# Two fused attentions: steps grouped in blocks of two, and the maxima's matmuls spread over seven places of a block

## What is computed

```python
# A: 8 heads, latent of 32, per head 128 + 32 dimensions
c_q = h @ W_DQ + b_DQ ; c_kv = h @ W_DKV + b_DKV
scores = einsum('bhsd,bhtd->bhst', q, k) * scale ; o = softmax(scores) @ v_c
A = o.reshape(b, s, 1024) @ W_O + b_O
# B: 16 heads of 16 dimensions, keys masked by a similarity to a global token
pos = sim > 0.9
x_pos = masked_attn(pos) ; x_neg = masked_attn(~pos)       # masked softmax
B = where(pos, x_pos, x_neg) @ W_proj + b_proj             # the first 5 tokens: their mean
```

## Time and profile before

| | us |
|---|---|
| median of 3 runs | 3412.9 (3410.66 to 3431.38) |
| span of the profiled execution | 3409.3 |
| PE busy | 3051.9 (90%) |
| DVE busy | 2265.2 (66%) |
| ACT busy | 1709.1 (50%) |
| POOL busy | 1060.2 (31%) |
| PE waiting for DVE's maxima, at the maxima of B (L1008) | 75.9 in matmuls, 309.2 in weight loads |

### The profile page before, as it was taken

One profiled execution on the slowest core, in us unless ns is written; L12 is line 12 of the kernel. 1 busy time (PEld: TensorE's weight loads), 2 busy tenths in 40 slices (PEclk: granted clock), 3 DMA queues, 4 the chain that ended last, 5 costly groups with the idle time before them and its releaser, 6 DMA issues.

```text
span 3409.3 us, 47004 instructions
## 1 busy us (share of the span) xinstructions
PE 3051.9 (90%) x17538; PEld 1327.5 (39%) x17538; DVE 2265.2 (66%) x4088; ACT 1709.1 (50%) x1948; POOL 1060.2 (31%) x552
## 2 busy tenths in 40 slices
PE   5538898999989998999989998999989999899997
PEld 4423433344333433344333433344333433344333
DVE  4435466776767667776767667776767667676782
ACT  1211354654555454654555454654555455654565
POOL 1021451235222451235222451235222451235201
PEclk8765999999999999999999999999989999999998
DMA  3212421450034201450034301450034201550001
GB/s 116 89 49 69 95 52 41 106 107 17 28 83 99 60 22 47 106 104 18 28 83 97 62 19 50 105 105 18 28 83 96 64 18 37 117 107 15 19 15 33
DMA packets 130051, 213.54 MB, mean 63 GB/s; under 512 B 48376, under 2 KB 76952, under 8 KB 129688
## 3 DMA queue, kind: packets, MB, share of 16 engines
q1 hardware_dynamic: 125480, 202.24, 24.9%
q10 hardware_dynamic: 4352, 8.39, 0.7%
HBM read 137.28 MB, written 73.02 MB: 62 GB/s over the span
## 4 chain that ended last, share of the span: by engine, by line
PE 75%; DVE 16%; issue 3%; DMA 3%; POOL 2%; ACT 1%; SPq 0%; DVEq 0%; POOLq 0%; ACTq 0%
PE O L1104 22%; PE M L1008 14%; DVE mx L1310 13%; PE M L1002 8%; PE S L1092 7%; PE S L1089 4%; PE M L1028 3%; PE M L1118 3%; PE M L1069 2%; PE M L974 2%; PE M L1037 2%; PE M L1071 2%; PE M L1024 1%; DMA kt_d<-stg 1%; PE M L1033 1%
## 5 line engine op out<-in xcount | busy, mean ns | idle before, releaser
L1310 DVE TENSOR_REDUCE mx<-M 128x1 f32<-128x512 f32 x3072 | 1975.6, 683 | 742.0 <-PE M L1008 443.8
L862 ACT ACTIVATE PT<-S 128x1024 f32<-128x1024 f32 x1280 | 1269.1, 1023 | 881.7 <-PE S L1092 572.9
L1008 PE MATMUL M<-KB,QB 50*128 50x512 f32 x2048 | 684.2, 488 | 129.4 <-DVE mx L1310 75.9
L1008 PEld LDWEIGHTS M<-KB,QB 50*128 50x128 f32 x2048 | 281.2, 189 | 796.2 <-issue 395.6
L1104 PE MATMUL O<-PT,VB 128*32 128x512 f32 x4096 | 562.9, 622 | 0.7 <-ACT PT L862 0.7
L1092 PE MATMUL S<-QB,KB 52*128 52x512 f32 x2048 | 527.1, 448 | 2.4 <-ACT PT L862 2.1
L1002 PE MATMUL M<-KA,QA 98*128 98x512 f32 x1024 | 449.8, 479 | 38.8 <-DVE mx L1310 15.5
L746 POOL TENSOR_TENSOR PT<-PT 128x2048 f32<-128x2048 f32 x64 | 292.2, 4566 | 381.9 <-PE O L1104 364.7
L862 ACT ACTIVATE PTx<-S 128x1024 f32<-128x1024 f32 x256 | 248.5, 1022 | 249.0 <-PE S L1089 248.9
L746 POOL TENSOR_TENSOR PTx<-PTx 128x2048 f32<-128x2048 f32 x64 | 292.2, 4566 | 228.8 <-PE O L1104 228.8
L1002 PEld LDWEIGHTS M<-KA,QA 98*128 98x128 f32 x1024 | 182.8, 195 | 352.6 <-issue 193.4
(11 more groups left out here) (146 smaller groups left out, 1940.0 us busy)
## 6 DMA issues: line engine op xcount, KB each, us to landing
qk_d<-stg SPq DMA_DIRECT2D x32, 1024.0 KB
KA<-kt_d SPq DMA_DIRECT2D x48, 512.0 KB, 7.3
QB<-qk_d SPq DMA_DIRECT2D x192, 128.0 KB
KB<-qk_d SPq DMA_DIRECT2D x192, 128.0 KB
kt_d<-stg SPq DMA_DIRECT2D x16, 1024.0 KB
RB<-recb_d SPq DMA_DIRECT2D x64, 256.0 KB
PT<-in_x SPq DMA_DIRECT2D x16, 512.0 KB, 3.8
xn_d<-xnT ACTq DMA_DIRECT2D x16, 512.0 KB, 2.8
```

The costliest lines, as they stand in the source:

```text
L862: nc.scalar.activation(probs(kind, of_a)[:, 2 * pair:2 * pair + 2, :], Sg[pair][:, :].rearrange("p (j s) -> p j s", j=2), ACT.Exp, scale=S ...
L1008: done = mm(m[:, :], QB[rows, 2 * q + a, at:at + P], KB[rows, 2 * q + a, keys], start=True, stop=True)
L1310: v.tensor_reduce(mx[:, g % 2, unit, kh:kh + 1], m[:, :], AX.X, ALU.max).then_inc(free, 1)
```

## The change

The loops run over blocks of two steps (RUN = 2). A block's part list has seven places; its eight maxima are spread over them by SPREAD, for all four stages alike: u0 and u1 ahead of the first scores, u2, u3, u4 each ahead of one further pair of scores, u5 ahead of the first values, u6 and u7 between the two values, none at the end. PE's order in a block is

```diff
+RUN = 2
+SPREAD = ((0, 2), (2, 3), (3, 4), (4, 5), (5, 6), (6, 8))
+MID = 2
 def place(s, at, kind, nxt):
     units = max_units(kind, nxt)
-    for i in range(NC):
-        step, (u0, u1, u2, u3) = s[at + i], units[4 * i:4 * i + 4]
-        ...
+    for i in range(NC // RUN):
+        u = units[4 * RUN * i:4 * RUN * (i + 1)]
+        for part, (lo, hi) in enumerate(SPREAD):
+            s[at + i][part] = u[lo:hi] + s[at + i][part]
...
-THREE = 3
+THREE = 2 // RUN
...
-    def probs(kind, k):
-        if kind == "a":
-            return (PT if k % 4 < 2 else PTx)[:, k % 2]
-        return PT[:, k % 2]
+    def probs(k):
+        return (PT if k % 4 < 2 else PTx)[:, k % 2]
...
         def add_pair(n, i):
             k = 2 * i + 1
-            wait_apart(pool, pv_done, n * STEPS + k)
+            if n or i:
+                wait_apart(pool, dn_done, n * PAIRS + i)
             wait_apart(pool, e_done, n * (2 * STEPS) + (2 * k + 2))
-            to = probs("a", k - 1)
-            nc.gpsimd.tensor_tensor(to, to, probs("a", k), ALU.add).then_inc(summed, 1)
+            nc.gpsimd.tensor_tensor(SUM[:, :, :], probs(k - 1), probs(k), ALU.add).then_inc(summed, 1)
...
         def b_steps(b, last):        # ACT
-            for k in range(STEPS_B):
-                exps(b, STEPS_A + k, "b")
-                if k == 0:
-                    take_out(b, "a", GA - 1)
-                ...
-                fills(sum(slots[k], []), lambda j: b_spot(b, last, j), b + 1)
+            for d in range(BLOCKS_B):
+                fills(slots[d][0], lambda j: b_spot(b, last, j), b + 1)
+                for i in range(2 * RUN):
+                    exps(b, STEPS_A + RUN * d + i // 2, "b", i % 2)
+                    fills(slots[d][i + 1], lambda j: b_spot(b, last, j), b + 1)
+                ...
+                if d == 0:
+                    take_out(b, "a", GA - 1)
...
-            for e in range(2):
+            for e in ((0, 1), (1, 0))[pair]:
...
         def b_steps(b, last):        # PE
-            for k in range(STEPS_B):
-                scores(b, k, "b", 0)
-                some(k, 0)
-                scores(b, k, "b", 1)
-                some(k, 1)
-                if k:
-                    values(b, k - 1, "b")
-                ...
-                some(k, 2)
+            for d in range(BLOCKS_B):
+                for i in range(2 * RUN):
+                    some(d, i)
+                    scores(b, RUN * d + i // 2, "b", i % 2)
+                for i in range(RUN):
+                    some(d, 2 * RUN + i)
+                    if d:
+                        values(b, RUN * (d - 1) + i, "b")
+                    ...
+                if RUN * (d + 1) == 2:
+                    denominators(b, b, PAIRS - 1)
+                some(d, PARTS - 1)
```

More of the change, by code:

```diff
@@ L97, in jobs_b @@
-    if more:
[L98 to L102, removed]
+            s[(g * NC + 1) // RUN][MID].append(("fa", "a", 0))
+    s[6 // RUN][MID] += [("rs", 0), ("rs", 1)]
+    s[10 // RUN][MID] += [("rt", 0), ("rt", 1)]
+    s[12 // RUN][MID] += [("rv", 0)]
+    for c, at in enumerate((44, 46, 52, 54)):
+        s[at // RUN][MID].append(("po", c))
@@ L103, in jobs_b @@
+    if more:
+        s[14 // RUN][MID] += [("lat", 0), ("lat", 1)]
+        s[18 // RUN][MID] += [("va", 0)]
+        for at, name in ((20, "kt0"), (24, "kb"), (28, "kt1"), (34, "qk0"), (40, "qk1"), (48, "qk2"), (58, "qk3")):
+            s[at // RUN][MID].append((name, 0))
+            s[(at + 2) // RUN][MID].append((name, 1))
     for g in range(GB):
         if g + 2 < GB:
-            place(s, g * NC, "b", g + 2)
+            place(s, g * GROUP, "b", g + 2)
         elif more:
-            place(s, g * NC, "a", g + 2 - GB)
+            place(s, g * GROUP, "a", g + 2 - GB)
@@ L583, in load_z @@
                 wait_apart(sp, ld_b[q], b * LD_B + LD_B)
-            wait_apart(sp, z_clear, b + 1)
+            if b:
+                wait_apart(sp, sr_ready, b)
             for e in range(2):
@@ L642, in b_steps @@
             for g in range(GB):
+                if g + 1 < GB:
+                    shift(b, "b", g + 1, b_spot(b, last, ("fa", "b", g + 1)))
+                elif not last:
+                    shift(n, "a", 0, b_spot(b, last, ("fa", "a", 0)))
                 if g:
@@ L646, in b_steps @@
                     dens(b, "a", GA - 1)
-                if g + 1 < GB:
-                    shift(b, "b", g + 1, b_spot(b, last, ("fa", "b", g + 1)))
-                elif not last:
-                    shift(n, "a", 0, b_spot(b, last, ("fa", "a", 0)))
                 if g == 0:
@@ L1135, in some @@
                     job(j, a_spot(n, b, j), b if j[0] == "po" else n, b)
-            for k in range(STEPS_A):
-                scores(n, k, "a", 0)
-                some(k, 0)
-                scores(n, k, "a", 1)
-                some(k, 1)
-                if k:
-                    values(n, k - 1, "a")
-                elif before:
-                    values(b, STEPS_B - 1, "b")
-                if k >= 3 and k % 2 == 1:
-                    denominators(n, b, (k - 3) // 2)
-                some(k, 2)
+            for d in range(BLOCKS_A):
+                for i in range(2 * RUN):
+                    some(d, i)
+                    scores(n, RUN * d + i // 2, "a", i % 2)
+                for i in range(RUN):
+                    some(d, 2 * RUN + i)
+                    if d:
+                        values(n, RUN * (d - 1) + i, "a")
+                    elif before:
+                        values(b, STEPS_B - RUN + i, "b")
+                if RUN * d >= 2 and RUN * (d + 1) % 2 == 0:
+                    denominators(n, b, RUN * (d + 1) // 2 - 2)
+                some(d, PARTS - 1)
         def b_steps(b, last):
@@ L1175, in _ @@
         b_steps(B - 1, True)
-        values(B - 1, STEPS_B - 1, "b")
+        for i in range(RUN):
+            values(B - 1, STEPS_B - RUN + i, "b")
         for j in TAIL:
```

161 lines of the change are left out of this document (70 added, 91 removed).

## The result

| | before | after |
|---|---|---|
| median of four runs each, us | 3414.2 (3410.66 to 3431.38) | 3495.3 (3486.36 to 3498.34) |
| ratio, 95% interval | | 1.0226 (1.0197 to 1.0254) |
| span of the profiled execution, us | 3409.3 | 3495.5 |
| TensorE's granted clock, mean over the span (the view of cores) | 0.945 | 0.929 |

The changed kernel is slower by 2.3%. The time lies inside the forecast range, and slower had the largest chance, but the forecast was 3444: of the 82 us above the 3412.9 that it started from, 31 were forecast.

What follows compares the result with a forecast made beforehand. PE held 75% of the chain; in B/b a PE-DVE loop was the bound. Full batch -10.3 + 7.0 + 6.0 + 0.6 = +3.3, seven times +23, last +10.6: +34 on 3412.9 is 3446, taken as 3444; range 3350 to 3510.

Steps and rivals of the forecast that it cites:

- The plain B/b block: B/b blocks without a job: two exponentials in a row set 5.92 us, for 5.86 before, +0.06 a block.
- the plain block of B/a: B/a: added changes of tile shape take two steps from 5.98 to 6.86 us, +0.88 a block, +7.0 a batch.
- The rival of cheap changes: B/a and A/b: a lone matmul costs 0.23, not 0.44, so both stages stay even; 3347 us, chance 0.1.
- that of DVE as the bound: B/b: exponentials overlap better, a block falls to DVE's 4.96 and a little, 5.3; 3330 us, chance 0.1.
- the sum of B/b: B/b in a full batch: plain blocks, job places, fa, start of B and kb stall together -10.3 us.
- -0.43 a job place: B/b: PE's idle time hides part of each job, saving 0.43 us at 15 places, 6.5 a batch.
- -0.35 an fa: B/b: each of six transposes fa vanishes in the wait, saving about 0.35 us, 2.0 a batch.
- -1.2 at B's start: Start of B: maxima further apart, so the missing bank no longer costs; some -1.2 us a batch.
- -2.0 at kb: B/b: kb's eviction waits for kt0's store; DVE reaches the reciprocal about 1.4 us earlier, taken as -2.0.
- J + 5.11: B/b: V1 to V1 of a block with a job of length J, so J - 0.81 over a plain 5.92.
- the jobs are not covered: B/b: a projection's eviction on ACT delays the block's later exponentials, losing the 6.5 and 2.0; 3508 us, chance 0.2.
- The last batch: Final batch: B/b -4, A +6.6, tail of 8 blocks without maxima +8 (4.9 us a block), together +10.6 us.

Runs made afterwards that it cites:

- half exponentials: Changed kernel with B's exponentials over half of the columns, the values reading that half twice: 3448.6 us in one run.
- The repeats: Changed kernel with maxima u3 and u4 computed twice in B's blocks that hold no job but a transpose: 3464.4 us, 1.0142.
- The job ahead of u3: Changed kernel with the job moved from behind u3 to ahead of it in the blocks of B that hold B's maxima: 3501.9 us, 1.0226.
- the jobs behind S11: Changed kernel with all jobs moved from the third place in a block to the fifth, ahead of the first values: 3638.7 us in one run.
- The two reordered queues: kt0's store and load_a put ahead of recs in B's group 2: changed kernel 3512.4 us, 1.0275; kernel before 3438.4 us, 1.0056.
- the side parts alone: Kernel before, in single steps, with ring of four, tile SUM, Z cleared once, shift ahead of dens, scratch of 1024: 3423.5 us, 1.0018.

## Why the prediction was right or wrong

**Right, with its numbers.** The plain B/b block (5.92 forecast, 5.91), S11 behind V1 (3.82, 3.82) with ACT as its releaser, the plain block of B/a (6.86, 6.86), that of A/b (8.3, 8.26), and near them the windows of A/b (71, 69.5) and B/a (66, 65.0). A/a gave -1.1 where +0.6 was forecast. By the Trainium skill (TensorEngine Tiling (Array Packing), Key Properties) each change of tiling mode drains the engine, and full rows and 64 rows are two modes; the trace agrees that such a change has a price, a lone maximum or pair of scores costs 0.43. The rival of cheap changes is refuted by the same rows, and that of DVE as the bound by ACT as releaser; only with half exponentials does the block come to 5.32, about the 5.3 that this rival named, with DVE busy for 5.10 of it. The rule on the most contended engine (the Trainium skill, Perfetto Trace Analysis, Identifying the Most-Contended Engine) pointed to DVE; in the changed kernel it misled, because a loop through two engines set the block and no engine was full.

**The step that failed** is the sum of B/b: "24 x 0.06 = +1.4, -6.5, -2.0, -1.2, -2.0 = -10.3". It was +1.3, 11.6 apart in each full batch, and it falls into three parts.

The table has the 24 blocks in five groups: their mean over the six middle batches, each block at its shortest in any of them, and the forecast by the prediction's own terms (+0.06 a block, -0.43 a job place, -0.35 an fa, -1.2 at B's start, -2.0 at kb).

| blocks | mean before | mean after | shortest before | shortest after | shortest, change | forecast |
|---|---|---|---|---|---|---|
| B's start (3 blocks) | 20.8 | 23.2 | 20.8 | 20.0 | -0.8 | -1.4 |
| rs, rt, rv, lat (5) | 45.1 | 44.0 | 43.8 | 43.2 | -0.6 | -1.8 |
| va, kt0 (4) | 29.6 | 30.4 | 28.2 | 28.9 | +0.7 | -1.4 |
| kb, kt1 (4) | 34.7 | 34.5 | 33.8 | 31.9 | -1.9 | -3.0 |
| qk0, qk1, po (8) | 56.8 | 56.1 | 56.4 | 55.7 | -0.7 | -2.8 |
| sum | 186.9 | 188.2 | 182.9 | 179.6 | -3.3 | -10.3 |

So the 11.6 are 7.0 that the order itself did not give, and 4.6 by which the blocks lie further above their shortest than before (8.5 instead of 4.0). Of these 4.6, 3.2 are at the start of B, whose three blocks took from 20.0 to 28.0 us, and 1.7 in the blocks of kb and kt1; those from rs to lat gave 0.5 back.

1. *The clock: 4.6 of spread, and some 3 more in rv and va.* The prediction said "In the third to sixth place PE now stands idle for about 1.7 us" and gave those waits no price beyond themselves. In batch 2 the low-clock time of B/b is 2 x 0.06 x 183.3 = 22 us and in batch 5 2 x 0.12 x 192.9 = 46, where the earlier trace rows have 2 x 0.04 x 185.2 = 15. Over the whole kernel it is 496 against 375: 121 us more, by the estimate of 0.37 to 0.39 each 45 to 47 of the 86. The repeats show it by experiment: work put into the waits took 31 us off. Two blocks meet the low clock in nearly every batch, that of rv and that of va; here they are in batch 2, after and then before:

```profile
1316.10:1328.00 11.90, 9.49 (x291) 4.85 (x288) 6.13 (x17) 3.87 (x4) 0.00 (x0) 0.71 0.01 3
1342.90:1354.80 11.90, 11.72 (x67) 6.67 (x64) 5.43 (x10) 3.83 (x4) 1.27 (x1) 0.71 0.22 59
```

```profile
1303.30:1314.50 11.20, 8.41 (x290) 4.99 (x291) 6.49 (x15) 4.06 (x4) 0.00 (x0) 0.90 0.01 3
1331.20:1340.30 9.10, 9.01 (x65) 5.60 (x65) 5.49 (x11) 3.94 (x4) 1.28 (x1) 1.00 0.32 77
```

The clock was 0.71 in both, 0.90 and 1.00 before. At their shortest they are 1.3 and 1.6 above their forecast; that this is the clock is worked out from its price, no experiment parts it from the order. That waits inside the blocks let the clock fall is shown as far as the repeats go; which wait does it in a given batch is not.

2. *The job places, some 2.8 us.* "J + 5.11" came out 0.20 to 0.25 longer (a qk block 7.11 for 6.91, a kt block 6.25 for 6.0): the lone u3 in front of the job takes 0.59, and not 0.43, where it has waited for its bank. The eight halves of kt and qk, with the fa in one of their blocks, missed 1.7 so, and the two blocks with po 1.1, most of it in the last block of the stage. The job ahead of u3 gave 2.1 back in the last eight blocks, all that they had missed, and little in kt's. Why a slot that has waited is dearer stays open. The rival "the jobs are not covered" is wrong as such: a projection's block costs 1.2 over a plain one, under its bound of 1.3, and the kernel with the jobs behind S11 shows what no cover costs.

3. *The stall at kb and B's start.* kb's block and the one behind it came from 21.8 to 21.1 in the mean, -0.7 for -2.0; at their shortest -1.7. The 1.4 of the earlier reciprocal came in full. At B's start -0.8 came at full clock for -1.4. These are the small ones, about 0.5 each. The two reordered queues show that the place behind recs is what kt0's store is late by, and that this place is a chain of stores, loads and evictions: in the changed kernel what kb won, kt1 lost.

The parts 2 and 3 and the 2.9 us of rv and va make 6.8 of the 7.0; each is worked out from single blocks and good to a few tenths.

**The last batch** was +17.5 and not +10.6. Its A stages gave +3.1 (forecast +6.6), B/b +3.3 (-4), the tail +11.1 (+8). A tail block at full clock is:

```profile
3439.99 1.92 PE L1094 MATMUL O<-PT,VB 128*32 128x512 f32 x16
...
3443.53 0.50 PE L1082 MATMUL S<-QB,KB 52*128 52x512 f32 x2 [0.95 <-ACT PT L844]
3444.44 0.49 PE L1082 MATMUL S<-QB,KB 52*128 52x512 f32 x2 [0.41 <-ACT PT L844]
3444.86 1.92 PE L1094 MATMUL O<-PTx,VB 128*32 128x512 f32 x16
```

4.87 from values to values (forecast 4.9), with two waits for ACT in it; the others of the eight are up to 6.5 at the lower clock. The clock over this batch is 0.92 (before 0.96), 32 us more of low clock and so about 12 us. In the kernel with the repeats its B/b is 160.0, 3.6 under the kernel before, about as forecast, and the tail +9.2. A plain block of the tail at full clock went from 4.0 to 4.9, by 0.9 and not 1.1, so the excess in the tail is not its order.

**The setup** was +4.1 (334.4 against 330.3 to the first exponential), where the prediction had nothing: clearing Z once, 1.06 us on POOL in the setup, was called free without looking at who waits for POOL there. With the side parts alone the setup is 331.9, 1.6 over before. The other 2.5 us were not followed up.

**The range** held the time, but its upper end, 3510, was set by uncovered jobs, and another cause brought the time near it.

## What to carry to other kernels

When an edit leaves the bound where it is but cuts a stage's waits into pieces inside each block, or makes them longer, price the clock too: read the granted clock of the stage before, and ask where PE's new waits lie. A matmul of another tile shape between two of the same costs a change on both sides, so small work is best placed in pairs beside its like. And an order with a long chain of evictions and stores behind a single staging tile is judged by the sum of its stalls over some blocks, not by the one that an edit removes.

## What was not expected of the hardware

- The same four blocks took 30.0 us at a granted clock of 1.00 and 38.0 at 0.73, in one execution. One microsecond at the lower clock cost 0.37 to 0.39 us here, less than the 0.5 that a stretch of PE without waits would lose.
- Two repeated matmuls a block in a wait made the kernel 31 us faster (3495.3 to 3464.4); the same kind of repeat in the kernel before, also in a wait but where the plain blocks already ran at full clock, made it 0.24% slower.
- Shortening blocks at full clock (7.11 to 6.82) was paid back by the clock and a longer stall: low-clock time 496 to 554 us, the stall's two blocks 1.4 us longer, and no gain at all.
- A lone matmul slot that had waited for its bank cost 0.59 to the next tile shape, one that had not, 0.43.
